# Order lists for three engines, S^T in four row groups, 32-row window scores, and half of a SiLU rebuilt on ScalarE and GpSimd

## The reference

```
m = silu(cond) @ W_mod + b_mod                     # shifts, scales, gates
h = LN(x) modulated;  x += gate * (self-attention(h) @ W + b)
h = LN(x) (modulated in L1);  x += [gate *] (cross-attention(h, context) @ W + b)
h = LN(x) modulated;  x += gate * (mlp(h) @ W + b)
```

## Time and profile before

| what | value |
|---|---|
| median of three timed executions | 476.36 us |
| the profiled execution, its span | 460.53 us, 458.7 us |
| TensorE busy | 374.1 us (82%) |
| VectorE busy | 297.2 us (65%) |
| ScalarE busy | 204.3 us (45%) |
| GpSimd busy | 111.9 us (24%) |
| mean granted TensorE clock | 0.851 |
| chain that ended last, by engine | PE 57%, DVE 29%, ACT 7%, issue 5% |

### The profile page before, as it was taken

The page is one execution under the profiler, slowest core; times in us unless marked ns, Lnnn a source line. Parts: engine busy times, 40 slices in busy tenths (PEclk is TensorE's granted clock), DMA queues, the critical chain, the costliest instruction groups (busy, mean ns, idle before and its releaser), DMA issues.

```text
span 458.7 us, 8982 instructions
## 1 busy us (share of the span) xinstructions
PE 374.1 (82%) x3317; PEld 210.5 (46%) x3317; DVE 297.2 (65%) x1279; ACT 204.3 (45%) x303; POOL 111.9 (24%) x130
## 2 busy tenths in 40 slices
PE   3999899999989987899888889978574566675985
PEld 2325412223333155677655567754353344454454
DVE  4648556999897056666338361235989999997342
ACT  1311126666756935666432123332453555653511
POOL 5332304910010011001015100011434544444010
PEclk9965659999999999999999585566877877776999
DMA  7544625110000000000000000000000000000000
GB/s 201 37 157 120 186 59 156 53 55 2 3 1 2 0 1 1 1 2 1 1 1 2 4 1 7 3 3 1 1 1 1 2 2 1 1 1 1 1 24 24
DMA packets 13247, 12.88 MB, mean 28 GB/s; under 512 B 2373, under 2 KB 11681, under 8 KB 13203
## 3 DMA queue, kind: packets, MB, share of 16 engines
q1 hardware_dynamic: 13007, 12.28, 10.3%
q0 software_dynamic: 160, 0.01, 0.0%
q10 hardware_dynamic: 36, 0.01, 0.0%
HBM read 9.41 MB, written 2.63 MB: 26 GB/s over the span
## 4 chain that ended last, share of the span: by engine, by line
PE 57%; DVE 29%; ACT 7%; issue 5%; POOL 1%; DMA 1%; SPq 0%; ACTq 0%; DVEq 0%; POOLq 0%
PE psum L1491 6%; PE psum L1561 5%; PE psum L1529 5%; DVE left L1284 4%; DVE left L1291 4%; PE psum L1514 4%; DVE mx L1210 4%; PE psum L1355 3%; PE psum L1660 3%; DVE top L1281 3%; DVE top L1288 3%; PE psum L1508 3%; PE psum L1485 2%; PE psum L1544 2%; PE psum L1628 2%
## 5 line engine op out<-in xcount | busy, mean ns | idle before, releaser
L1210 DVE TENSOR_REDUCE mx<-psum 128x1 f32<-128x512 f32 x128 | 81.4, 684 | 26.4 <-PE psum L1491 18.0
L803 ACT ACTIVATE big<-psum 128x1024 f32<-128x1024 f32 x64 | 62.5, 1022 | 46.1 <-PE psum L1514 25.2
L607 POOL TENSOR_TENSOR rstd<-vareps,minus_half 128x4 f32<-128x4 f32 x12 | 12.2, 1020 | 178.8 <-DVE vareps L969 178.7
L1561 PE MATMUL psum<-kblk,qf 128*128 128x308 f32 x128 | 46.0, 490 | 1.1 <-DVE qf L1157 0.8
L1572 PE MATMUL psum<-ident,pr 128*77 128x128 f32 x256 | 38.3, 299 | 10.5 <-POOL pr L725 10.5
L1491 PE MATMUL psum<-KS,QS 72*128 72x512 bf16 x112 | 43.0, 417 | 3.0 <-DVE mx L1210 2.3
L1572 PEld LDWEIGHTS psum<-ident,pr 128*77 128x77 f32 x256 | 34.4, 167 | 18.4 <-POOL pr L725 13.9
L725 POOL TENSOR_TENSOR pr<-pr,early 128x616 f32<-128x616 f32 x16 | 23.9, 1493 | 55.8 <-ACT early L909 37.8
L1529 PE MATMUL psum<-big,V 128*9 128x512 f32 x256 | 34.3, 609 | 0.5 <-ACT big L803 0.5
L1584 PE MATMUL psum<-QS,vc 77*9 77x128 f32 x256 | 13.9, 342 | 24.1 <-ACT QS L919 24.0
L1514 PE MATMUL psum<-QS,KS 75*128 75x512 bf16 x112 | 32.8, 379 | 0.4
(11 more groups left out here) (202 smaller groups left out, 687.3 us busy)
## 6 DMA issues: line engine op xcount, KB each, us to landing
QS<-scr_q SPq DMA_DIRECT2D x7, 288.0 KB
KS<-scr_k SPq DMA_DIRECT2D x7, 288.0 KB
scr_q<-qp SPq DMA_DIRECT2D x2, 384.0 KB, 2.9
scr_k<-kp SPq DMA_DIRECT2D x2, 384.0 KB, 3.6
gates<-scr_g SPq DMA_DIRECT2D x2, 320.0 KB, 4.1
early<-in_L_xcond_w_ada_dram SPq DMA_DIRECT2D x1, 576.0 KB, 5.1
scr_k<-kp SPq DMA_DIRECT2D x2, 256.0 KB, 4.3
wmlp<-in_L_xcond_W_mlp_dram SPq DMA_DIRECT2D x2, 256.0 KB, 3.2
```

What stands on the lines that cost most here:

```text
L803: freed(act.activation(pT[:, u % 2, 1024 * half:1024 * (half + 1)], ps, ACT.Exp), "sT", 0, u, half)
L1210: freed(dve.tensor_reduce(mx[:, n % 3, at:at + 1], ps, AX_X, ALU.max), "max", t, q)
L1561: last = pe.matmul(ps[:, 512 * a:512 * a + HH // 2 * S], qf[:, b, i * P:(i + 1) * P], kb[:, c0:c0 + HH // 2 * S], start=True, stop=True)
```

## The change

The loops of L0's cross-attention and of all of L1 are replaced by three explicit lists (`pe_order`, `dve_order`, `act_order`) that every engine walks. L0's cross-attention keeps its order. What is different is the following.

- The modulation and gate work of L0's steps 4 to 6 moves to steps 9, 10, 11 and 13, into the rooms of the row maxima. `spread_gates` goes behind `max_rows` of group 2 in SyncE's queue, and GpSimd's `gate_outputs` therefore later.
- S^T of units 0 to 3 is issued with both halves one after the other, instead of with a row maximum between them.
- Window maxima and scores read 32 rows instead of 8 and 9; the added rows hold zeros.
- Batch 1's window projections stand between batch 0's maxima, and batch 1's maxima between batch 0's windows. Batch 1's scores use only room W1, L1's cross scores only W0.
- Batch 0's MLP of L1 is issued inside the cross loop (e = 13, 14); the two other halves of a pair of chunks share one two-bank room. Its SiLU becomes tanh and a halved linear part on ScalarE, and a sum and a product on GpSimd. Batch 1's SiLU stays.
- Batch 0's `mlp_out` stands before batch 1's last turn and projection. L1's cross divides come half a tile earlier. Some tiles move to other SBUF places.

```diff
-EARLY = {0: ("ln",), 1: ("qk",), 2: ("v0",), 3: ("v1",), 4: ("ctx", "m01"), 5: ("kv", "gate0"), 6: ("mods", "gate1")}
+EARLY = {0: ("ln",), 1: ("qk",), 2: ("v0",), 3: ("v1",), 4: ("ctx",), 5: ("kv",), 9: ("m01",), 10: ("gate0",),
+         11: ("mods",), 13: ("gate1",)}
...
+def first_halves(j, q):
+    if not 0 <= j < UNITS:
+        return ()
+    if j < NT:
+        return (0, 1) if q == 1 else ()
+    return (q,) if q < 2 else ()
...
+    order += [("wqk", 0, c) for c in range(NQ)] + pieces("wv0 max000 max001 lnT31")
+    order += [("wqk", 1, 0)] + pieces("max010 max011") + [("wqk", 1, 1)] + pieces("max020 max021")
+    order += [("wqk", 1, 2)] + pieces("max030 max031") + [("wqk", 1, 3)] + pieces("mT0 wv1 max100 max101 max110")
+    order += pieces("S0 S1 V0 max111 S2 V1 W0 max120 S3 V2 W1 max121 max130 V3 W2 max131 W3 mT1 "
+                    "oT20 S4 out30 S5 V4 lnT40 S6 V5 W4 qc10 S7 V6 W5")
+    ahead = {0: "V7 W6", 1: "W7", 10: "oT30", 13: "lnT50"}
+    behind = {2: "oT21", 3: "out31", 4: "lnT41", 5: "qc11", 10: "out40"}
+    for e in range(-1, HALVES + 1):
+        found, turns = cross_pieces(e, 1)
+        order += found + pieces(ahead.get(e, "")) + turns + pieces(behind.get(e, ""))
+        order += [("mlp1", 0, e - 13)] if e in (13, 14) else []
+    order += [("D", 1, B * NT - 1)] + pieces("out50 oT31 out41 lnT51") + [("mlp1", 1, 0), ("mlp1", 1, 1)] + pieces("out51")
...
+    order += pieces("max010 q10 max011 max020 q11 max021 max030 q12 max031 mT0 q13 v1 max100 max101 max110")
+    order += pieces("max111 W0 max120 W1 max121 max130 W2 max131 W3 mT1 res30 stat40 norm40 W4 qc10 W5")
+    inside = {2: "W7", 11: "res40 stat50", 12: "norm50"}
+    behind = {1: "W6", 3: "res31 stat41", 4: "norm41", 5: "qc11", 14: "gate00 gate01", 15: "gate02 gate03"}
+    for e in range(HALVES):
+        order += [("first8", e)] + pieces(inside.get(e, "")) + [("next8", e)]
+        if e % 2 and e >= 3:
+            order.append(("D", 1, (e - 3) // 2))
+        order += pieces(behind.get(e, ""))
+    order += [("D", 1, B * NT - 1)] + pieces("res50 res41 stat51 norm51 gate10 gate11 gate12 gate13 res51")
...
+            def hidden_silu(b, *chunks):
+                for c in chunks:
+                    pool.wait_ge(s_half, NC_ * b + c + 1)
+                    wait_read(pool, "mlp", 1, b, c)
+                    pool.tensor_scalar(sa[b][c % 2], sa[b][c % 2], 1.0, None, ALU.add).then_inc(s_tanh1, 1)
+                    pool.wait_ge(s_tanh1, c + 1)
+                    pool.tensor_tensor(sa[b][c % 2], sa[b][c % 2], sx[b][c % 2], ALU.mult).then_inc(s_silu, 1)
...
+                if e == 4:
+                    ln_rstd(4, 1)
+                if e == 14:
+                    hidden_silu(0, 0, 1)
+                if e == 15:
+                    hidden_silu(0, 2, 3)
+                if e == 11:
+                    ln_rstd(5, 0)
                 pool.wait_ge(s_ex, HALVES + 2 * (e + 1))
                 pool.tensor_tensor(pr[:, k, :], pr[:, k, :], taken[:, k, :], ALU.mult).then_inc(s_pr, 1)
...
+                    if c == 2:
+                        wait_read(act, "mlpb", b, 0)
                     if b:
+                        v = VECS["L1_b_m1"] + c
+                        freed(act.activation(sa[b][c % 2], ps, ACT.Silu, bias=cols[:, v:v + 1]), "mlp", 1, b, c)
+                        return
+                    act.activation(sx[b][c % 2], ps, ACT.Identity, scale=0.5, bias=half_cols[:, c:c + 1])\
+                        .then_inc(s_half, 1)
+                    freed(act.activation(sa[b][c % 2], ps, ACT.Tanh, scale=0.5, bias=half_cols[:, c:c + 1]),
+                          "mlp", 1, b, c)
...
-                                                     QF[q0:q0 + D, b, c, t0:t0 + WIN], KF[q0:q0 + D, b, c, t0:t0 + WIN],
+                                             QF[q0:q0 + QUAD, b, c, t0:t0 + WIN], KF[q0:q0 + QUAD, b, c, t0:t0 + WIN],
...
-                                                     KF[q0:q0 + DV, b, c, t0:t0 + WIN], QF[q0:q0 + DV, b, c, t0:t0 + WIN],
+                                                 KF[q0:q0 + QUAD, b, c, t0:t0 + WIN], QF[q0:q0 + QUAD, b, c, t0:t0 + WIN],
...
+            def gated_mlp_in(b, pair):
+                w = W["wm1"]
...
+                for c in (2 * pair, 2 * pair + 1):
+                    ps = open_room(pe, "mlp", 1, b, c)
+                    filled(pe.matmul(ps, w[:, c * P:(c + 1) * P], hT[:, b, :], start=True, stop=True), "mlp", 1, b, c)
+                ps = open_room(pe, "mlpb", b, pair)
+                for j in range(2):
+                    w0 = HID + (2 * pair + j) * P
+                    last = pe.matmul(ps[:, N * j:N * (j + 1)], w[:, w0:w0 + P], hT[:, b, :], start=True, stop=True)
+                filled(last, "mlpb", b, pair)
```

More of the change, by code:

```diff
@@ L92, with pieces, cross_pieces @@
 GATE_SPAN = ((0, 2), (2, 5))
+def pieces(text):
+    return [tuple([word.rstrip("0123456789")] + [int(d) for d in word[len(word.rstrip("0123456789")):]])
+            for word in text.split()]
+def cross_pieces(e, layer):
+    last = B * NT * 2
+    found = [("sc", layer, e + 1)] if e + 1 < last else []
+    turns = [("T", layer, e - 1)] if 1 <= e <= last else []
+    if e % 2 == 0 and 1 <= e // 2 <= B * NT:
+        turns.append(("C", layer, e // 2 - 1))
+    if layer == 0 and e % 2 == 0 and e >= 4:
+        turns.append(("D", layer, e // 2 - 2))
+    if layer == 1 and e % 2 and e >= 3:
+        turns.append(("D", layer, (e - 3) // 2))
+    return found, turns
@@ new lines, in rooms_in_turns @@
+    for t in range(STEPS):
+        j = t - LOOK - 1
+        for q in range(NT):
+            if t < HEADS:
+                use("Y", "max", t, q)
+            for half in first_halves(t - LOOK, q):
+                use("W", "sT", 0, t - LOOK, half)
+            if q == 1 and t % G == 0 and 1 <= t // G <= B * NG:
+                use("Y", "mT", 0, t // G - 1)
+            if q == 2 and j % NT == 0 and 0 <= j < UNITS:
+                use("M0", "pv", 0, j // NT)
+        for item in EARLY.get(t, ()):
+            for kind, key in EARLY_ROOMS[item]:
+                use(kind, *key)
+        if j > 0 and j % NT == 0:
+            use("Y", "pvT", 0, j // NT - 1)
+        for at, key in ((T_OUT, ("oT", 0, 0)), (T_OUT + 2, ("out", 0, 0)),
+                        (T_OUT + 5, ("lnT", 1, 0)), (T_OUT + 7, ("qc", 0, 0))):
+            if t == at:
+                use("Y", *key)
@@ L225, in room @@
             r, _ = TURN[key]
[L226 removed]
+            return psum[:, 512 * bank[r]:512 * (bank[r] + (2 if key[0] in ("sT", "sc", "maxw", "mlpb") else 1))]
         def row_groups(ps):
@@ L361, in build @@
         sa = [[qf[:, b, :], kf[:, b, :]] for b in range(B)]
+        sx = [[KF[:, b, j, :] for j in range(2)] for b in range(B)]
+        half_cols = sb("half_cols", [P, NC_])
         scr_q = nc.dram_tensor("scr_q", [B, 3 * D, H * N], BF16, kind="Internal").ap()
@@ new lines, in next_eight @@
+            def next_eight(e):
+                k, base = e % 2, 3 * HH * e
+                row = lambda t, h: t[:, k, S * h:S * (h + 1)]
+                for h in range(HH):
+                    dve.wait_ge(s_top, base + HH + h + 1)
+                    dve.max(top[:, k, h, 8:16], row(left, h)).then_inc(s_top, 1)
+                for h in range(HH):
+                    dve.wait_ge(s_top, base + 2 * HH + h + 1)
+                    ins_ = dve.match_replace(out=row(left, h), in_to_replace=top[:, k, h, 8:16],
+                                             in_values=row(left, h), imm_value=-BIG)
+                ins_.then_inc(s_left, 1)
@@ new lines, in window_pv @@
+            def window_pv(u):
+                b, i = steps[u]
+                ps = open_room(pe, "pv", 1, u)
+                if i == 0:
+                    wait_read(pe, "qkv", 1, b, "v")
+                for half in range(2):
+                    wait_read(pe, "sT", 1, u, half)
+                for h in range(H):
+                    c, j = divmod(h, NQ)
+                    p0 = HALF * j + WIN * c
+                    last = pe.matmul(ps[QUAD * j:QUAD * j + 2 * DV, c * WIN:(c + 1) * WIN],
+                                     VW[:, b, i, h, :, :].rearrange("p w e -> p (w e)"),
+                                     pT[:, u % 2, p0:p0 + WIN], start=True, stop=True)
+                filled(last, "pv", 1, u)
```

1029 lines of the change are left out of this document (478 added, 551 removed), and 6 rows, old and new, of the table EARLY_ROOMS.

## The result

The changed kernel is slower. Its 20 timed executions took 470.9 to 479.7 us, median 474.24; the ratio to the kernel before is 1.0325, with a 95% interval of 1.028 to 1.037. The profiled execution after took 477.9 us, its span 475.9 against 458.7.

What follows compares the result with a forecast made beforehand. Bounds were taken as TensorE before 76 and from 240 to 316 us, VectorE from 316 to 419, then a chain through all engines. Gains 7.5 + 3.5 + 1 = 12 us off 476.4 gave 464 us, range 452 to 476.

Steps and rivals of the forecast that it cites:

- Parts 1 and 2: L0's self-attention: moving work of steps 4 to 6 and pairing S^T halves gains 3.5 + 6.4 - 2.4 = 7.5 us.
- side by side: L0's first four S^T units: the second half runs beside the first at next to no cost, 6.4 us saved.
- the move: L0's modulation and gate work of steps 4 to 6 goes later: 3.5 us gained early, 2.4 paid back in steps 9 to 13.
- Part 3: L1's windows: batch 1's projections fill the waits on the maxima; 3.5 us gained, ends -4 and 14.
- Part 4, the loop: L1's cross loop on VectorE, with added gate products and norm: 1.5 + 1.1 + 1.1 - 1.5 = 2.2 us longer.
- The -1.5: L1's cross loop: VectorE's 2.0 us wait for batch 1's projection shrinks as earlier turns come half a tile sooner; 1.5 saved.
- The silu stall: L1's cross loop: VectorE waits about 1.1 us for GpSimd's second silu before a gate product.
- Part 4, the tail: After the last top-k: batch 0's MLP leaves TensorE, 8.2 - 3.7 - 0.6 - 0.75 = 3.1 us gained.
- The 0.6 for GpSimd's fourth pair: Tail: 0.6 us lost as GpSimd multiplies the last half only after its fourth silu.
- The base: The 15.8 us between the profiled execution (460.53) and the median of timed runs (476.4) stays unchanged.
- rival (c): L1's cross loop: GpSimd's sum is slow and delays gate and last products; 481.5 us with a 5 us sum; chance 0.09.
- My own mark: Sign of a wrong mechanism: stretch up to 163 not shorter by at least 4 us, or cross loop longer by over 4.

Runs made afterwards that it cites:

- c_early: c_best with the moved work of L0's steps 4 to 6 and the sending of the gate rows back in the old places; median 458.38 us.
- a_res: The changed kernel with VectorE's residual, statistics and norm of batch 0 in L0's cross-attention one half later, as before; median 469.29 us, ratio to before 0.993.
- c_w20: c_best with two added matmuls that nobody reads, ahead of TensorE's wait for batch 0's window maxima; median 458.18 us, ratio to the kernel before 0.999.
- c_best: The changed kernel with L1's cross-attention and tail in old order, batch 0's SiLU one ScalarE function, L0's batch 0 residual one half later; median 457.61 us.
- c_warm: c_best with unread matmuls ahead of TensorE's waits for the window maxima, two for batch 0 and three for batch 1; median 456.46 us.
- s_silu: The changed kernel with L0's residual, ScalarE's list and TensorE's window turns mended, and batch 0's SiLU as one ScalarE function; median 461.02 us.

## Why the prediction was wrong

- **Parts 1 and 2 (7.5 gained)** held as a sum: 6.3 in this trace, 8.4 with the mean of 13, both against one trace of before. The pieces were off, and that they made up for each other was luck: side by side 3.7 to 3.9 instead of 6.4, the move 2.0 (c_early, within the scatter) to 4.5 (8.4 less 3.9) instead of its net 1.1 (3.5 - 2.4). I had named the exponentials as the limit behind; it was TensorE's other work of a step.
- **L0's cross-attention** was priced at nothing, because I took its order as unchanged. That is the second step that failed: 7.2 us went there. One step of VectorE's list, one half too early, was 3.0 of them (a_res). Of the other 4.2 the clock after one stall makes 1.7, and the stage's length goes with its granted clock in all the traces (last section); no run takes the clock and the order apart there.
- **Part 3 (3.5 gained)** gave -0.1, inside its ends of -4 and 14. The wait in front of S4 was 3.45 instead of 4.9, and the scores ran at 0.50 as taken (269 to 312: 0.54). What I did not see is that the new order has the full clock at the stage's beginning (241 to 269: 0.99; in the kernel before 0.80 from the first projection to S0) and then the low one for most of the next 43 us, with batch 1's maxima among the scores. That the two cancel is read from the traces and was not tested.

```profile
294.21 1.13 PE L1712 MATMUL psum<-KS 32*64 32x64 f32 x32 [3.45 <-DMA KS<-mneg]
```

- **Part 4, the loop**, is the main step that failed: "The loop gets 1.5 + 1.1 + 1.1 - 1.5 = 2.2 longer". It got 13.3 longer. The -1.5 has the wrong sign: the wait for the residual of batch 1, to shrink "since the turns before it come half a tile earlier", grew from 2.0 to 6.67 together with that for the divide, which stood behind `oT21` and the turn of tile 7. The wait of 3.79 for `lnT50` is missing. The silu stall was 0.60 + 2.05 instead of 1.1, as the sum took 1.49 and not 0.65. The norm was 1.24 for 1.1. These four are 4.7 + 3.8 + 2.65 + 1.24 and, with 1.5 for the two gate products, 13.9 of the 13.3 us, so no other loss has to be looked for. The top-k beside GpSimd cost nothing, as priced: VectorE's busy time in the loop grew from 99.2 to 102.0 us, which is the added norm and products. I had followed what the change puts into VectorE's queue, and not what stands in front of whom in the lists of ScalarE and TensorE.
- **Part 4, the tail (3.1 gained)**: TensorE's work there fell from 29.43 to 26.50 us, but its clock from 0.91 to 0.76, and the last product of GpSimd stood behind the fourth pair until 435.46, 2.5 us after the last replacement instead of 0.9. It is -2.8 in this trace, +0.8 in `a_res` (39.3); the shortest tails are 39.3 with the new order and 39.8 with the old one (c_w20), so at most about 0.5 of the 3.1 came. The 0.6 for GpSimd's fourth pair was 1.6; how much each of the other terms missed is not shown.

The tail of the trace before, for comparison with the last row of the stage table above:

```profile
418.61:458.70 40.09, 29.43 (x164) 19.23 (x164) 14.16 (x35) 12.97 (x19) 5.04 (x4) 0.91 0.05 14
```

- **The base**: the 15.8 us between the profiled execution and the median, taken as unchanged without a row, did not stay. The profiled execution after took 477.9, 3.7 above its median. So 464 carried a distance that the kernel after does not have.
- **The chances**: 0.08 for slower came almost all from rival (c). Of (c) a stall of 2.65 came true, which decided nothing; most of the loss came from places in the lists, for which there was no rival. My own mark, "if the cross loop grows by more than 4", is what came.

## What to carry to other kernels

Where loops are rewritten as order lists, compare the lists of every engine step by step with the old order, also in the stages that the change is not about, and ask at each moved step what it waits for and what ready work stands behind it. A step that is moved forward in an in-order queue is a gain only if its input is there by then: here three edits of order, which put a few steps back by one place or one half tile, gave back 11 us, more than the 6 to 8 that the change saved in the first stage. Put small late steps (a residual, a turned norm) behind the recurring work of the loop, not ahead of it.

## What the runs showed of the hardware

On GpSimd adding 1.0 in place to 128x512 was not cheaper than a product with two inputs: 1.49 us on the average of four (1.50 in the row above), against 1.27.

In the windows the granted clock was 0.53 although TensorE was busy for 20.26 of 21.92 us, with matmuls of which three quarters (415 of 560 records) had 32 rows and 64 columns (`c_best`); with two large matmuls ahead of them the same small ones ran at 0.90 (`c_warm`). So in these runs they did not bring the clock back, but could run under it.

The same stall did not have the same consequence in both kernels. In L0's cross-attention TensorE is busy for 1.32 of 4 us in the trace before and in that after alike; the next 4 us had a granted clock of 1.00 before, and of 0.59 after. The rows, before and then after:

```profile
171.60:175.60 4.00, 1.32 (x33) 0.53 (x25) 3.90 (x10) 1.68 (x3) 2.05 (x2) 1.00 0.00 0
175.60:179.60 4.00, 4.00 (x26) 3.36 (x27) 2.37 (x4) 2.88 (x5) 0.24 (x1) 1.00 0.00 0
```

```profile
165.30:169.30 4.00, 1.32 (x33) 0.53 (x25) 3.90 (x10) 1.68 (x3) 2.06 (x2) 0.99 0.00 0
169.30:173.30 4.00, 4.00 (x16) 3.21 (x17) 1.96 (x3) 1.51 (x3) 3.46 (x6) 0.59 0.00 0
```

The lead of the trace after shrinks there from 6.31 to 4.65 us. The clock fell at this place in all 15 traces with the new lists; of the kernel before there is only the one trace. The length of the whole stage follows its mean granted clock: 1.00 in the trace before (76.5 us), 0.98 in `s_silu` and `c_early` (78.9), 0.96 in the seven other traces with the edit of `a_res` (80.5 to 80.9), and 0.94 in the six without it (83.7 to 83.9). Why the clock falls with the new lists and not before stays open; no run was made for it.
